# The front of a two-layer graph kernel: left sums as a column of H's products and laid out by DMA, normalisation on GpSimd, weights loaded from ScalarE's queue

## What is computed

```python
h = jnp.maximum(_layernorm(x, axis=-1), 0.0)
# first layer, on h (called x here)
type_sum_a = adj_a @ x; type_sum_b = adj_b @ x
attn_a = sigmoid(concatenate([type_sum_a, x], axis=1) @ Wa.T + ba)
attn_b = sigmoid(concatenate([type_sum_b, x], axis=1) @ Wb.T + bb)
h = x @ W_sa
s_left = h @ a_sa[0, :Hd]
s_right = h @ a_sa[0, Hd:]
scores = s_left[:, None] + s_right[None, :]
e = where(adj_a != 0, exp(-leaky_relu(scores, 0.01)), 0.0)
attn = e / (sum(e, axis=1, keepdims=True) + 1e-05)
x_a = attn @ h
x_b = adj_b @ (x @ W_gcnb) + b_gcnb
return sigmoid(attn_a * x_a + attn_b * x_b)
```

## Time and profile before

| | |
|---|---|
| median of 3 runs | 1592.4 us |
| the profiled execution | 1592.87 us |
| its span | 1591.0 us |
| TensorE busy | 1552.8 us (98% of the span) |
| VectorE, ScalarE, GpSimd busy | 1141.3, 1076.0, 969.0 us |
| front (iterations 0 to 12) | from 12.4 to about 101 us |

### The profile page before, as it was taken

How to read it: one execution, slowest core, us unless ns; L and a number is a source line. 1 busy time by engine, 2 the same in 40 slices (tenths; PEclk the granted TensorE clock), 3 DMA queues, 4 the chain that set the end, 5 groups by cost and what they waited for, 6 DMA issues and landing times.

```text
span 1591.0 us, 34868 instructions
## 1 busy us (share of the span) xinstructions
PE 1552.8 (98%) x12946; PEld 1539.3 (97%) x12946; DVE 1141.3 (72%) x2145; ACT 1076.0 (68%) x2129; POOL 969.0 (61%) x864
## 2 busy tenths in 40 slices
PE   6999999999999999999999999999999999999998
PEld 5999999999999999999999999999999999999997
DVE  7766666766675677777777777766777777777774
ACT  4579989988985566666666666655666666666666
POOL 2112222222220388888888888856888888888885
PEclk9999999999999999999999999999999999999999
DMA  4124444554441133333333334622333333333333
GB/s 149 48 61 120 121 119 115 128 140 116 119 102 34 37 97 100 100 101 100 97 99 99 100 100 133 204 83 68 100 100 101 100 101 101 101 102 103 101 101 107
DMA packets 88696, 163.36 MB, mean 103 GB/s; under 512 B 9295, under 2 KB 19406, under 8 KB 88270
## 3 DMA queue, kind: packets, MB, share of 16 engines
q1 hardware_dynamic: 60480, 113.26, 24.4%
q0 software_dynamic: 24336, 44.31, 11.4%
q10 hardware_dynamic: 3710, 3.56, 0.7%
HBM read 147.99 MB, written 13.11 MB: 101 GB/s over the span
## 4 chain that ended last, share of the span: by engine, by line
PE 83%; issue 6%; DVE 5%; POOL 3%; ACT 2%; DMA 0%; POOLq 0%; DVEq 0%; ACTq 0%
PE PS L1255 29%; PE PS L1467 8%; PE PS L1470 8%; PE PS L1469 8%; PE PS L1330 5%; PE PS L1327 5%; PE PS L1329 5%; PE PS L1328 5%; PE PS L1326 5%; POOL FR L474 2%; POOL X L467 1%; DVE AF L1071 1%; DVE AF L1003 1%; ACT FR L669 1%; DVE PS L1111 1%
## 5 line engine op out<-in xcount | busy, mean ns | idle before, releaser
L474 POOL TENSOR_TENSOR FR<-AF,FR 128x512 fp32r<-128x512 f32 x338 | 451.0, 1334 | 138.1 <-ACT FR L669 132.5
L1255 PE MATMUL PS<-FR,RB 128*128 128x256 f32 x3900 | 516.2, 281 | 1.8 <-ACT X L623 1.8
L1255 PEld LDWEIGHTS PS<-FR,RB 128*128 128x128 f32 x3900 | 481.8, 188 | 3.1 <-ACT X L623 3.0
L467 POOL TENSOR_TENSOR X<-X,ROW 128x512 f32<-128x512 f32 x283 | 371.0, 1311 | 82.0 <-ACT ROW L679 82.0
L1467 PE MATMUL PS<-FR,RA 128*128 128x256 f32 x1300 | 372.6, 287 | 7.2 <-POOL FR L474 5.6
L1470 PE MATMUL PS<-FR,RA 128*128 128x256 f32 x1300 | 365.1, 281 | 0.0
L1469 PE MATMUL PS<-FR,RA 128*128 128x256 f32 x1300 | 364.3, 280 | 0.0
L1071 DVE TENSOR_TENSOR AF<-PS,AJ 128x512 f32<-128x512 f32 x338 | 231.3, 684 | 79.9 <-ACT PS L635 68.9
L432 POOL DMA_DIRECT2D STGT<-adjt x169 | 90.1, 533 | 293.0 <-PE PS L1330 293.0
L623 ACT ACTIVATE X<-PS 128x512 f32<-128x512 f32 x272 | 161.7, 594 | 142.0 <-DVE AF L1003 136.1
L1467 PEld LDWEIGHTS PS<-FR,RA 128*128 128x128 f32 x1300 | 244.7, 188 | 13.2 <-POOL FR L474 11.6
(11 more groups left out here) (174 smaller groups left out, 2457.0 us busy)
## 6 DMA issues: line engine op xcount, KB each, us to landing
AJ<-adjt SPq DMA_DIRECT2D x338, 256.0 KB, 2.7
STGT<-adjt POOLq DMA_DIRECT2D x169, 256.0 KB, 3.0
xt_scratch<-ROW SPq DMA_DIRECT2D x12, 512.0 KB, 2.7
RB<-xt_scratch SPq DMA_DIRECT2D x12, 512.0 KB, 4.7
x_scratch<-X ACTq DMA_DIRECT2D x13, 256.0 KB, 2.1
ROW<-x_scratch SPq DMA_DIRECT2D x13, 256.0 KB, 3.1
out<-ROW SPq DMA_DIRECT2D x12, 256.0 KB, 3.3
X<-xt SPq DMA_DIRECT2D x1, 1536.0 KB, 11.1
```

Of the source, the lines that this page charges most:

```text
L467: nc.gpsimd.tensor_tensor(slot, slot, MB.unsqueeze(1).broadcast_to([P, 2, 256]), ALU.subtract)\
L474: nc.gpsimd.tensor_tensor(LO[g % 2], WA[g % 2], HI[g % 3].bitcast(F32), ALU.subtract)\
L1255: last = nc.tensor.matmul(out, stationary(a, k), moving(b, k), start=(k == 0 and i == 0), stop=(k == K - 1 and i == 2))
```

## The change

- **Left sums.** L is gone from the loop. The vector W_sa a_left becomes the fourth column beside H, so the left sums come out of H's product as a column, one number in each partition (`SL`, the fourth column of `XS`). For pairs 1 to 12 SyncE stores this column to a scratch in HBM, in pieces of one element, and loads it back to all partitions (`partition_broadcast`), in two parts: pairs 1 to 6 after H of pair 6, pairs 7 to 12 after H of pair 12. For pair 0, which units 0 to 12 use, ScalarE spreads the column (`spread_left`), TensorE turns it with two transposes in iteration 1 (`turn_left`), and ScalarE copies it out (`left_sums`). `leaky0(0)` and what follows it move to behind that, and `unit0(0)` waits for `sl_first`, since bank 1 is used by both.
- **Banks.** An iteration has 5 bank uses instead of 6; the turning of pair 1 goes to bank 0.
- **Normalisation.** From pair 2 on GpSimd normalises, ahead of the adjacency loads 6 to 14, which are issued one in an iteration.
- **Weights.** `wx` is issued by ScalarE, after pair 0 of x has landed. Its sums by VectorE (L932, L936) become copies by ScalarE with an accumulated output.
- **Order on VectorE.** Statistics of iterations 0 to 4 stand ahead of `h2_low`, scales behind the first `g_low`, the mask of unit 0 behind the statistics of iteration 1.

The core of the difference:

```diff
-            return 6 * pr + i + 1 if i else max(6 * pr - 5, 0)
+            return 5 * pr + i + 1 if i else max(5 * pr - 4, 0)
-            sp.dma_start(WRAW0[:, :, 0:GX + D + 2], wx).then_inc(w_in, 16)
+            for i, (p0, p1) in enumerate(SL_PARTS):      # SL_PARTS = [(1, 7), (7, PAIRS)]
+                sp.wait_ge(sr_done, 2 * p1)
+                sp.dma_start(sl_dram[2 * P * p0:2 * P * p1].rearrange("(t p o) -> p t o", p=P, o=1),
+                             SL[:, 2 * p0:2 * p1, :], allow_slow_non_contiguous=True).then_inc(sl_st, 16)
+                sp.wait_ge(sl_st, 16 * (i + 1))
+                sp.dma_start(SLB[:, 2 * P * p0:2 * P * p1],
+                             sl_dram[2 * P * p0:2 * P * p1].partition_broadcast(P)).then_inc(sl_in[i], 16)
# GpSimd
+            normalise(2)
+            for p in range(1, PAIRS - 2):
+                if p - 1 in LN_CHAIN:
+                    i = LN_CHAIN[p - 1]
+                    inverse_root(i, *LN_PARTS[i])
+                normalise(p + 2)
+                if p >= 2:
+                    load_unit(p - 2 + NSTG)
# ScalarE
+            act.wait_ge(x_in[0], 16)
+            act.dma_start(WRAW0[:, :, 0:GX + D + 2], wx).then_inc(w_in, 16)
+            for side in range(2):
+                act.wait_ge(wv_pool, side + 1)
+                c = GX + D + 3 - side
+                for k in range(K):
+                    wa = (PEB, PAB)[side][:, k, 0:D]
+                    last = nc.scalar.activation(wa, wa, ACT.Copy, accum_out=WRAW0[:, k, c:c + 1])
# TensorE
-                if p >= 1:
-                    products_l(p)
                 products_g(p)
                 if p == 0:
                     transpose0(1)
-                    pe.wait_ge(w_ready, 2)
-                    products_l(0)
+                    pe.wait_ge(w_ready, 1)
+                if p == 1:
+                    turn_left()
                 products_h(p)
...
+            def turn_left():
+                pe.wait_ge(sl_spread, 1)
+                for h in range(2):
+                    last = nc.tensor.transpose(PS[:, 1, h * P:(h + 1) * P], PEB[:, h, 0:P], IDN[:, :])
+                last.then_inc(sl_mm, 1)
```

More of the change, by code:

```diff
@@ L196, in two_graph_blocks @@
         wv_zero = sem("wv_zero")
-        wv_step = sem("wv_step")
-        wsl_hi = sem("wsl_hi")
+        wv_done = sem("wv_done")
+        sl_spread = sem("sl_spread")
+        sl_mm = sem("sl_mm")
+        sl_first = sem("sl_first")
+        sl_st = sem("sl_st")
+        sl_in = [sem(f"sl_in{i}") for i in range(len(SL_PARTS))]
         wh_cast = sem("wh_cast")
@@ L437, in inverse_root, with normalise @@
                 nc.gpsimd.tensor_tensor(LNT[:, 1, t0:t1], LNT[:, 0, t0:t1], NHALF[:, 0:t1 - t0], ALU.pow)                  .then_inc(ln_pow, 1)
+            def normalise(pr):
+                pool.wait_ge(ln_done, next(i for i, (t0, t1) in enumerate(LN_PARTS) if 2 * pr + 1 < t1) + 1)
+                if pr:
+                    pool.wait_ge(tp_done, pr)
+                for h in range(2):
+                    t = 2 * pr + h
+                    last = nc.gpsimd.tensor_scalar(HN[:, h, :], X[:, t, :], RSTD[:, t:t + 1], NMR[:, t:t + 1],
+                                                   ALU.mult, ALU.add)
+                last.then_inc(hn_done, 1)
             pool.wait_ge(half_set, 1)
@@ L451, in _ @@
                 load_unit(n)
-            for n in range(2, len(LN_PARTS)):
-                inverse_root(n, *LN_PARTS[n])
-            for n in range(UN - NSTG):
+            normalise(2)
[6 more added lines that the diff above has]
+                    load_unit(p - 2 + NSTG)
+            for n in range(PAIRS - 4, UN - NSTG):
                 pr, k = n // UNITS - 1, n % UNITS
@@ L510, in leaky0 @@
                 pr, u = n // UNITS, n % UNITS
-                act.wait_ge(slb_done, pr + 1)
+                if pr == 0:
+                    act.wait_ge(sl_first, 1)
+                else:
+                    act.wait_ge(sl_in[next(i for i, (p0, p1) in enumerate(SL_PARTS) if pr < p1)], 16)
                 act.wait_ge(sr_done, 2 * u + 2)
@@ L923, in _ @@
             normalise(0)
+            dve.wait_ge(x_in[1], 16)
+            statistics(2, 4)
             dve.wait_ge(wg_hi, 1)
@@ L947, in _ @@
                     transposed_low(p + 1)
+                g_low(p, 0)
                 if p - 1 in LN_CHAIN:
@@ L950, in _ @@
                     scales(i, *LN_PARTS[i])
-                if 1 <= p < PAIRS - 2:
-                    normalise(p + 2)
-                g_low(p, 0)
-                if p >= 1:
+                if p >= 2:
                     mask0(p - 1)
@@ L958, in _ @@
                     transposed_low(1)
-                    normalise(2)
-                h2_low(p, 0)
-                if p >= 1:
-                    low0(p - 1)
-                h2_low(p, 1)
                 if p in LN_STATS:
@@ L969, in _ @@
                     statistics(t0, t1)
+                if p == 1:
+                    mask0(0)
+                h2_low(p, 0)
+                if p >= 1:
+                    low0(p - 1)
+                h2_low(p, 1)
                 if p in LN_CHAIN:
                     i = LN_CHAIN[p]
-                    variances(i, *LN_PARTS[i], 2 + sum(b <= LN_PARTS[i][1] for a, b in LN_STATS.values()))
+                    variances(i, *LN_PARTS[i], 3 + sum(b <= LN_PARTS[i][1] for a, b in LN_STATS.values()))
             mask0(UNITS - 1)
@@ L1294, in products_g @@
                 for h in range(2):
[L1295 to L1296 removed]
+                    projected(turn(pr, 1 + h))
+                    product3(PS[:, bank_of(pr, 1 + h), 0:GX], lambda a, k: ht[:, a, k, h * P:(h + 1) * P],
                              lambda c, k: WX[:, c, k, 0:GX]).then_inc(g_mm, 1)
+            def turn_left():
+                pe.wait_ge(sl_spread, 1)
+                for h in range(2):
+                    last = nc.tensor.transpose(PS[:, 1, h * P:(h + 1) * P], PEB[:, h, 0:P], IDN[:, :])
+                last.then_inc(sl_mm, 1)
             def products_h(pr):
@@ L1307, in unit0 @@
                 pr, u = n // UNITS, n % UNITS
+                if n == 0:
+                    pe.wait_ge(sl_first, 1)
                 if u == 0 and pr == 1:
```

96 lines of the change are left out of this document (43 added, 53 removed).

## The result

The changed kernel takes 1590.17 us (median of 20 runs), the kernel before beside it 1593.3: a ratio of 0.9982, 95% interval 0.9976 to 0.9989. It is faster by 3.1 us. The forecast was 1581.0, with a range from 1577.5 to 1586.5, so it failed by 9. The profiled execution took 1589.82 with a span of 1588.0, against 1592.87 and 1591.0: 3.05 less. The kernel before comes in two groups, near 1591.9 and near 1593.4 us: of its 77 ordinary executions beside the experiments, all 36 with a mean granted clock of 0.998 took 1593.06 or more and all 16 with 1.000 took 1592.92 or less, so that up to 1.5 us between two medians can come from the clock and not from an edit.

A forecast was written before the change was run, and what follows sets the result against it. TensorE was taken to bound the kernel, holding 83% of the chain of waits. Terms of +0.2, -6.3, -5.6 and +0.3 summed to -11.4, taking 1592.4 to 1581.0 us, range 1577.5 to 1586.5.

The forecast's parts named there:

- Part 1: The start, up to iteration 1's T: the later weights eat what the start saves, +0.2 us, bounds -2.6 to +4.9.
- the half share: At the start: the weights share the DMA engines half and half with x and land at 8.6 us.
- W: Landing time of the weights at the start, taken as 10.0 us, with bounds 7.2 and 14.7.
- rival A: At the start: small weight pieces lose against x's large ones, landing at 12 to 14.7; 1583 to 1585.7 us, chance 0.16.
- Part 2: Iterations 1 to 5: -6.3 us, from -3.75 of TensorE's own work and -2.6 of waits.
- The walk: Iterations 1 to 5 stepped through in the new order with old durations: 30.4 us together, of which waits 4.4.
- Part 3: Iterations 6 to 12: TensorE is full, so 0.80 us goes from each, 5.63 left an iteration, -5.6 in all.
- Rival B: Iterations 1 to 12: other engines or the port keep the loop; 1590.4 us, or 1586 if half; chance 0.15.
- Part 4: Behind the front: the wait of 2.0 us before unit 12 stays, 2.0 to 2.5, costing +0.3.
- Rival C: Left sums by DMA: 4-byte pieces make unit 13 wait, slower than before; 1648 us at 1 us a piece, chance 0.03.
- The port: GpSimd's lock against VectorE instructions with two SBUF inputs: by that rule collisions cost VectorE at most 0.6 us each.

The follow-up runs named there:

- e2: Changed kernel with the 1024 and 1536 KB parts of x held back until the weights, still issued by ScalarE, have landed: 1584.27 us, ratio 0.9948.
- e11: Kernel before with only the weights' load moved to ScalarE, issued after pair 0 of x has landed: 1600.54 us, ratio 1.0051.
- e1: Changed kernel with the weights issued by SyncE right behind pair 0 of x, as before the change: 1583.8 us, ratio 0.9945.
- e5: Changed kernel with the normalisation of pairs 2 to 12 back on VectorE: 1594.28 us, ratio 1.0007.
- e9: Changed kernel with high and low parts of the next unit put first on ScalarE and VectorE, units 12 to 18: 1589.31 us, ratio 0.998.
- e10: Changed kernel with both the edit of e1 and the order of e9: 1583.7 us, ratio 0.9941.
- e12: e10 with the second column store (pairs 7 to 12) put off until 39 leaky relus are done: 1587.74 us, ratio 0.9967.

## Why the prediction was wrong

**Part 1, the failed step.** "I take 10.0, between the half share and 11.0." The measured W is 14.66, the upper bound of the text (14.7) and rival A's end, to which I gave 0.16. The argument against A ("516 KB are a sixth of what is outstanding") took bytes for the share. e2 and e11 show that the company decides, and the packets that it does so by turns of one packet of 2 KB against one of 12 KB, behind a first packet that came 4.3 us after the issue. The sentence with the landing at 11.0 by such turns fails too: the trace has the turns, and with them the last packet of `wx` ends at 14.17. The chain behind W was right within a us. Term: +3.87 instead of +0.2, 3.7 of the 8.4 that are missing in the profiled execution. "Each us of W is a us of the time" held only in part: from e2 to the changed kernel 7.0 of W are 6.8 at unit 12, but e11 pays 7.5 for 9.2.

**Part 2, right in kind, 0.75 too large.** TensorE's busy time fell by 3.95 (32.23 to 28.28), forecast 3.75; its idle time fell by 1.6 and not by 2.6; it was 4.47 before by the earlier trace rows, not the 7.0 that the sum of the pieces left. The walk gave 30.4; e1, whose start is near that of before, has 30.30, the changed kernel 31.15. e5 confirms that the normalisation on GpSimd is part of it. GpSimd's normalisation was sized rightly: 0.57 a tile against this, by source line (ns min/median/max), though a pair costs TensorE 1.4 in iteration 2, which the walk had not.

```profile
L459 POOL TENSOR_SCALAR AF<-X,LNT x22: 544/556/1115, 22.2 to 79.8; 128x256 f32<-128x256 f32 x22
```

**Part 3, mis-sized by 1.3 of 4.8.** Four of the six iterations take 5.72 to 5.76 instead of 5.63, iteration 6 takes 5.82: the 24 products last 3.12 to 3.21 in the rows, against 3.04 before, gaps too short to be shown as waits. One, iteration 7, takes 6.33: VectorE's mask of unit 5 stood behind the last scales (which ended at 59.45), ScalarE waited 2.35 for it, and the second `h2_low` of iteration 6 began 1.87 after the T of iteration 7 (62.18 against 60.31), where in iteration 8 it is 0.66. Rival B is out as a bound: VectorE is busy 3.87 of 5.75, and no mask and hardly a low part of a unit is stretched (ns min/median/max):

```profile
L916 DVE TENSOR_TENSOR AF<-AF,STGT x169: 676/692/695, 29.4 to 478.1; 128x512 f32<-128x512 f32 x169
L922 DVE TENSOR_TENSOR FR<-AF,FR x169: 677/686/805, 30.8 to 482.1; 128x512 fp32r<-128x512 f32 x169
```

**Part 4, mis-sized by 0.7.** With L's 0.8 in iteration 12 the forecast was -0.5; the trace has +0.24. All of the 0.8 turned into waits and 0.24 more came: 0.6 before unit 12 (1.95 to 2.53, at the top of the forecast's 2.0 to 2.5), 0.3 before unit 11, the rest in gaps too short to be shown. This iteration is ended by the chain over ScalarE and VectorE, not by TensorE. No term had what followed: the lower clock behind the longer wait, +1.3. e9, e10 and e12 show that the chain can be shortened by 1.3, and that the column's store then takes the gain unless it is cut up.

**The rest**, +0.58, arises further on, of it 0.3 between 630 and 670 us, where the diff changes nothing. It was not followed, and its cause is open.

**Rival C** did not come: done by 79.6 (load issued at 72.85, 6.7 to landing), before unit 13 wanted it. The store's 10.9 us (median of the two) is beyond my 5 to 10, which priced the packets at 48 to 103 ns; they took 8, and the time went by behind them. The Trainium skill (DMA: Bandwidth & Descriptors, Rules for kernel authors) says that a last dimension that is not contiguous becomes one descriptor for each element. The trace agrees: 3327 packets under 512 bytes from 60 to 115 us with the column, 255 with rows, 3072 apart, twice 1536. Its price did not show as a late left sum, where I looked, but as late adjacency loads, e12 above all.

**The port.** VectorE's low part of G's weights took 1.06 at 15.33, against 1.58 at 8.09 in the kernel before, and ended 0.55 behind the end of GpSimd's product both times (15.84 and 9.12). The bounds W + 1.9 and W + 3.0 for its end were both above it: it ended at W + 1.7.

```profile
15.33 1.06 DVE L977 TENSOR_TENSOR WX<-AJ,WX 128x516 fp32r<-128x516 f32 x1 [7.36 <-ACT WX L605]
```
